# A gated delta rule layer with a mixture of experts on one core: gathers moved, GpSimd's first split behind the normalization, the last group's blocks sent earlier, new item orders in five iterations

## The reference

```python
St = St * jnp.exp(g_t)[..., None, None]
v_old = jnp.einsum('bhk,bhkv->bhv', k_t, St)
delta = (v_t - v_old) * b_t[..., None]
St = St + k_t[..., None] * delta[:, :, None, :]
o = jnp.einsum('bhk,bhkv->bhv', q_t, St)
```

## Time and profile before

| | |
|---|---|
| median of 3 runs | 1122.37 us (1120.64 to 1122.48) |
| the profiled execution | 1124.22 us |
| its span, first to last instruction | 1122.5 us |
| mean granted TensorE clock | 0.977 |
| PE busy | 1032.2 us (92%), 8190 matmuls |
| DVE busy | 809.2 us (72%) |
| ACT busy | 633.6 us (56%) |
| POOL busy | 524.9 us (47%) |
| the chain that ended last | PE 45%, DVE 10%, POOL 7%, ACT 5%, issue 5%, DMA 4% |

### The profile page before, as it was taken

The page is one execution under the profiler, slowest core; times in us unless marked ns, Lnnn a source line. Parts: engine busy times, 40 slices in busy tenths (PEclk is TensorE's granted clock), DMA queues, the critical chain, the costliest instruction groups (busy, mean ns, idle before and its releaser), DMA issues.

```text
span 1122.5 us, 22257 instructions
## 1 busy us (share of the span) xinstructions
PE 1032.2 (92%) x8190; PEld 791.8 (71%) x8190; DVE 809.2 (72%) x1469; ACT 633.6 (56%) x1176; POOL 524.9 (47%) x1140
## 2 busy tenths in 40 slices
PE   3999999987579999999999999999999999996987
PEld 3787666655367868677777878677777777684866
DVE  4632243429769898989888898989898888888444
ACT  2521222316537677676767676776767675674532
POOL 3331000006876465473837474563838383635620
PEclk9999999999869999999999999999999999998979
DMA  9941110014162423334152434234251524232121
GB/s 329 387 141 56 57 46 31 19 41 158 41 165 37 124 39 121 48 112 96 63 121 57 104 73 123 45 115 73 87 120 39 121 63 110 60 95 43 32 37 47
DMA packets 183513, 103.16 MB, mean 92 GB/s; under 512 B 155632, under 2 KB 169584, under 8 KB 180080
## 3 DMA queue, kind: packets, MB, share of 16 engines
q1 hardware_dynamic: 181872, 97.55, 31.7%
q0 software_dynamic: 1536, 4.20, 1.3%
HBM read 79.77 MB, written 21.95 MB: 91 GB/s over the span
## 4 chain that ended last, share of the span: by engine, by line
PE 45%; DVE 10%; POOL 7%; ACT 5%; issue 5%; DMA 4%; SPq 1%; DVEq 0%; ACTq 0%; POOLq 0%
PE rg L1512 7%; DVE nm L1276 5%; PE rg L1495 5%; PE rg L1479 4%; PE pj L1372 4%; PE pj L1373 4%; PE pj L1374 4%; POOL rows L1083 3%; POOL rows L1080 3%; PE rg L1487 2%; PE rg L1413 2%; PE rg L1496 2%; DVE shared_down_or_conv L1239 2%; ACT vn L1211 2%; ACT sqk L1165 2%
## 5 line engine op out<-in xcount | busy, mean ns | idle before, releaser
L1080 POOL TENSOR_TENSOR rows<-rows,shared_down_or_conv 128x126 f32<-128x126 f32 (+22 forms) x496 | 190.9, 385 | 240.5 <-DMA shared_down_or_conv<-n_scratch 202.8
L1239 DVE SCALAR_TENSOR_TENSOR shared_down_or_conv<-pj,taps,shared_down_or_conv 128x510 f32<-128x510 f32 x372 | 275.3, 744 | 26.4 <-ACT shared_down_or_conv L1128 17.5
L1083 POOL TENSOR_TENSOR rows<-rows 128x126 f32<-128x126 f32 (+22 forms) x496 | 197.0, 397 | 38.9
L1372 PE MATMUL pj<-xhi,whi 128*128 128x512 f32 x376 | 165.4, 440 | 7.6 <-DVE shared_down_or_conv L1239 3.9
L1276 DVE SCALAR_TENSOR_TENSOR nm<-rg,wneg,hidden_or_decays 128x512 f32<-128x512 f32 (+1 forms) x256 | 139.2, 608 | 16.4 <-PE rg L1415 16.2
L1373 PE MATMUL pj<-xlo,whi 128*128 128x512 f32 x376 | 150.7, 401 | 0.0
L1374 PE MATMUL pj<-xhi,wlo 128*128 128x512 f32 x376 | 150.5, 400 | 0.0
L1128 ACT ACTIVATE shared_down_or_conv<-pj,taps 128x512 f32<-128x512 f32 x124 | 85.3, 688 | 112.4 <-PE pj L1374 110.3
L1512 PE MATMUL rg<-wo,gated 128*128 128x256 f32 x512 | 132.2, 394 | 0.2 <-DVE nm L1276 0.2
L1512 PEld LDWEIGHTS rg<-wo,gated 128*128 128x128 f32 x512 | 95.4, 194 | 16.0 <-issue 2.2
L1372 PEld LDWEIGHTS pj<-xhi,whi 128*128 128x128 f32 x376 | 72.1, 192 | 46.5 <-issue 26.4
(11 more groups left out here) (216 smaller groups left out, 2033.8 us busy)
## 6 DMA issues: line engine op xcount, KB each, us to landing
hidden_or_decays<-eg_scratch SPq DMA_DIRECT2D x16, 1536.0 KB, 8.4
wraw<-w_heads SPq DMA_DIRECT2D x16, 776.0 KB, 4.4
w1a<-w_up SPq DMA_DIRECT2D x10, 1024.0 KB, 9.6
shared_down_or_conv<-n_scratch SPq DMA_DIRECT2D x32, 256.0 KB, 4.0
w2a<-w_down SPq DMA_DIRECT2D x8, 512.0 KB, 13.1
wo<-w_out SPq DMA_DIRECT2D x16, 256.0 KB, 2.7
n_scratch<-nm SPq DMA_DIRECT2D x64, 64.0 KB
rt_scratch<-shared_down_or_conv SPq DMA_DIRECT2D x32, 128.0 KB, 2.3
```

The costliest lines, as they stand in the source:

```text
L1080: gp.tensor_tensor(tmp, rb[:, 0:r, t:t + 1].to_broadcast([P, r, w]), nb[:, t:t + 1, t + 1:].to_broadcast([P, r, w]), ALU.mult).then_inc(el ...
L1083: gp.tensor_tensor(rb[:, 0:r, t + 1:], rb[:, 0:r, t + 1:], tmp, ALU.add).then_inc(elim, 1)
L1239: v.scalar_tensor_tensor(out=y, in0=it.pbank[item][:, :, 0:S - s], scalar=taps[par][:, piece(j)[0], KS - 1 - s:KS - s], in1=y, op0=ALU.mul ...
L1372: te.matmul(bank, whi[par][w], xhi[:, k, cols], start=(k == 0), stop=False)
```

## The change

1. POOL's first `split` waits for the end of DVE's normalization.
2. The 16 gathers go 5 ahead of `split_lo` of iteration -1, 3 behind it (ahead of elimination(0)), and 8 in iteration 0 behind `split_lo`, with the wait for all of them ahead of elimination(1).
3. SP's `blocks_out` is cut in two: the four writes (`blocks_out`) and the wait with the two fetches (`blocks_over`). In iteration NG - 2 the writes of group NG - 1 are issued inside `blocks_back(NG - 2)`, between `turned_back` and the wait ahead of `rows_back`. Elsewhere the order stays.
4. Iterations -1, 0, NG - 3, NG - 2 and NG - 1 get new lists of items for PE, ACT and DVE.

```diff
--- before.py
+++ after.py
@@ -303,6 +303,8 @@
                         gp.wait_ge(w_hi, s + 1)
                         if s:
                             gp.wait_ge(u_full, s * NS // ES)
+                        if s == 0:
+                            gp.wait_ge(dve, DVE_XN)
                         gp.tensor_tensor(w1lo[:], w1a[:, E - ES + s], w1hi[:].bitcast(F32), ALU.subtract).then_inc(w_lo, 1)
 
                     split(0)
@@ -852,37 +854,37 @@
             TAIL = {"SO", "OUT"}
             OWN = {
                 -1: (
-                    ("K0 K1 P4 K2 K3 P5 P6 P7 P0 P1 VT0 P2 VT1 VT2 P3 VT3").split(),
-                    ("P4 P5 W S4 P6 S5 SK P7 S6 P0 S7 P1 VT0 S0 P2 S1 P3 VT1 VT2 S2 S3 VT3").split(),
+                    ("K0 K1 K2 K3 P4 P5 P6 P7 P0 P1 VT0 VT1 VT2 P2 VT3 P3").split(),
+                    ("W P4 P5 S4 P6 S5 SK P7 S6 P0 S7 P1 S0 VT0 P2 VT1 S1 P3 VT2 VT3 S2 S3").split(),
                     ("K0 K1 K2 K3 P4 P5 P6 P7 P0 P1 P2 P3").split(),
                 ),
                 0: (
-                    ("P4 Z0 Z1 SQ P5 Z2 K0 Z3 P6 K1 P7 K2 K3 LA1 LA2 LB1 P0 LB2 P1 U1_0 U1_1 N21_0 N21_1 P2 U2_0 U2_1 "
-                     "VT0 P3 O0 O1 VT1 O2 O3 VT2 VT3").split(),
-                    ("E0 P4 Z0 SQ S4 P5 E1 Z1 P6 E2 E3 Z2 S5 SK W S6 LA1 P7 LA2 Z3 S7 LB1 LB2 P0 U1_0 U1_1 P1 U2_0 S0 "
-                     "U2_1 P2 S1 VT0 P3 O0 O1 VT1 O2 S2 S3 O3 VT2 VT3").split(),
-                    ("D0 D1 P4 D2 SQ P5 D3 K0 P6 K1 K2 K3 P7 MIX P0 N21_0 N21_1 P1 P2 P3 O0 O1 O2 O3").split(),
+                    ("Z0 Z1 P4 P5 SQ Z2 K0 P6 Z3 K1 K2 P7 P0 LA1 K3 LA2 LB1 P1 LB2 U1_0 U1_1 N21_0 N21_1 P2 U2_0 U2_1 "
+                     "VT0 P3 O0 VT1 O1 VT2 O2 O3 VT3").split(),
+                    ("E0 Z0 P4 SQ Z1 S4 P5 S5 E1 P6 E2 W Z2 E3 SK S6 Z3 P7 LA1 LA2 S7 LB1 LB2 U1_0 U1_1 P0 P1 S0 U2_0 P2 "
+                     "U2_1 VT0 S1 O0 P3 O1 VT1 O2 S2 O3 VT2 S3 VT3").split(),
+                    ("D0 P4 D1 D2 P5 SQ D3 K0 P6 K1 K2 P7 K3 MIX N21_0 N21_1 P0 P1 P2 O0 P3 O1 O2 O3").split(),
                 ),
                 NG - 3: (
-                    ("SO P4 Z0 SQ K0 K1 OUT0 Z1 Z2 Z3 OUT1 P5 OUT2 OUT3 LA1 P6 P7 K2 K3 LA2 OUT4 P0 LB1 OUT5 P1 LB2 P2 "
-                     "U1_0 OUT6 U1_1 N21_0 N21_1 U2_0 U2_1 OUT7 VT0 P3 O0 O1 VT1 O2 VT2 O3 VT3").split(),
-                    ("SQ P4 Z0 SO E0 E1 Z1 Z2 S4 W P5 Z3 S5 E2 P6 LA1 P7 E3 LA2 SK LB1 S6 P0 LB2 U1_0 S7 P1 U1_1 U2_0 S0 "
-                     "P2 S1 U2_1 VT0 O0 P3 S2 VT1 O1 O2 VT2 O3 VT3 S3").split(),
-                    ("SO D0 D1 SQ P4 K0 K1 D2 OUT0 P5 OUT1 OUT2 OUT3 D3 K2 K3 P6 P7 OUT4 OUT5 P0 OUT6 N21_0 N21_1 P1 P2 "
-                     "OUT7 O0 P3 O1 O2 O3").split(),
+                    ("SO Z0 P4 Z1 SQ Z2 K0 OUT0 K1 OUT1 Z3 OUT2 P5 P6 P7 LA1 K2 OUT3 LA2 K3 LB1 OUT4 OUT5 LB2 P0 OUT6 "
+                     "U1_0 U1_1 N21_0 P1 N21_1 U2_0 P2 U2_1 P3 VT0 OUT7 VT1 O0 O1 O2 O3 VT2 VT3").split(),
+                    ("SQ Z0 E0 Z1 P4 Z2 E1 SO Z3 P5 W E2 LA1 S4 E3 LA2 P6 LB1 S5 LB2 P7 S6 U1_0 P0 U1_1 SK S7 P1 U2_0 S0 "
+                     "P2 S1 U2_1 P3 VT0 VT1 S2 O0 O1 O2 O3 VT2 S3 VT3").split(),
+                    ("D0 SO D1 SQ P4 K0 OUT0 OUT1 D2 K1 D3 OUT2 P5 K2 OUT3 K3 P6 OUT4 OUT5 P7 OUT6 N21_0 P0 N21_1 P1 P2 "
+                     "OUT7 P3 O0 O1 O2 O3").split(),
                 ),
                 NG - 2: (
-                    ("P4 Z0 SO SQ K0 K1 Z1 K2 OUT0 K3 P5 LA1 P6 OUT1 LA2 OUT2 OUT3 OUT4 LB1 OUT5 OUT6 LB2 P7 Z2 Z3 U1_0 "
-                     "OUT7 U1_1 N21_0 N21_1 U2_0 U2_1 VT0 VT1 VT2 O0 O1 O2 O3 VT3").split(),
-                    ("P4 E0 SQ SO E1 E2 S4 E3 P5 Z0 Z1 LA1 P6 S5 LA2 LB1 S6 LB2 P7 U1_0 S7 SK U1_1 U2_0 U2_1 Z2 O0 VT0 "
-                     "VT1 O1 VT2 Z3 O2 O3 VT3").split(),
-                    ("D0 P4 SO D1 SQ D2 K0 K1 D3 K2 K3 OUT0 P5 OUT1 OUT2 P6 OUT3 OUT4 P7 OUT5 OUT6 OUT7 N21_0 N21_1 O0 "
+                    ("P4 Z0 SO SQ Z1 P5 K0 K1 K2 K3 LA1 Z2 OUT0 P6 OUT1 OUT2 Z3 OUT3 OUT4 LA2 P7 LB1 OUT5 OUT6 LB2 U1_0 "
+                     "U1_1 N21_0 N21_1 OUT7 U2_0 U2_1 VT0 VT1 O0 O1 O2 VT2 VT3 O3").split(),
+                    ("P4 SQ SO E0 Z0 E1 S4 Z1 P5 E2 E3 LA1 S5 P6 Z2 Z3 LA2 SK LB1 LB2 U1_0 U1_1 U2_0 P7 S6 U2_1 S7 VT0 "
+                     "O0 O1 VT1 O2 VT2 VT3 O3").split(),
+                    ("D0 D1 SO P4 SQ D2 D3 K0 K1 K2 K3 P5 OUT0 P6 OUT1 OUT2 OUT3 OUT4 OUT5 OUT6 N21_0 N21_1 P7 OUT7 O0 "
                      "O1 O2 O3").split(),
                 ),
                 NG - 1: (
-                    ("Z0 Z1 Z2 SO OUT0 OUT1 OUT2 OUT3 LA1 OUT4 LA2 OUT5 LB1 OUT6 OUT7 LB2 Z3 U1_0 U1_1 N21_0 N21_1 U2_0 "
+                    ("Z0 SO Z1 Z2 OUT0 OUT1 OUT2 OUT3 LA1 OUT4 LA2 OUT5 OUT6 LB1 OUT7 LB2 Z3 U1_0 U1_1 N21_0 N21_1 U2_0 "
                      "U2_1 O0 O1 O2 O3").split(),
-                    ("Z0 SO Z1 LA1 LA2 LB1 Z2 LB2 U1_0 U1_1 U2_0 U2_1 O0 Z3 O1 O2 O3").split(),
+                    ("SO Z0 Z1 LA1 LA2 LB1 LB2 U1_0 U1_1 U2_0 U2_1 Z2 O0 O1 Z3 O2 O3").split(),
                     ("SO OUT0 OUT1 OUT2 OUT3 OUT4 OUT5 OUT6 OUT7 N21_0 N21_1 O0 O1 O2 O3").split(),
                 ),
                 NG: (
@@ -985,6 +987,8 @@
                         rows_of = nm[par][C32 * q:C32 * (q + 1)].rearrange("p b e -> p (b e)").rearrange("p (m s) -> p m s", s=EC)
                         sp.dma_start(n_dram[:, q].rearrange("m i x -> i m x"), rows_of[:, :, first:first + C32]
                                      ).then_inc(blocks_out_sem, 16)
+
+                def blocks_over(n):
                     at_least(sp, blocks_out_sem, 64, n, 64)
                     at_least(sp, rt_out, 32, n, 0)
                     for h in range(2):
@@ -1014,6 +1018,8 @@
 
                     turned_back(0, t64[0:C32, :, :, 0:HR], turned_in)
                     turned_back(2, tc2, turned_in)
+                    if n == NG - 2:
+                        blocks_out(n + 1, 1 - it.odd)
                     sp.wait_ge(r_out, 32 * n + 32)
                     rows_back(1, back_odd)
                     rows_back(3, back_odd)
@@ -1030,7 +1036,9 @@
                     if "LA1" in it.items_a:
                         blocks_back(b, it)
                     if "K3" in it.items_v:
-                        blocks_out(b + 1, 1 - it.odd)
+                        if b != NG - 2:
+                            blocks_out(b + 1, 1 - it.odd)
+                        blocks_over(b + 1)
                         if "W" in it.items_a:
                             load_decays(b + 2)
                     if "OUT7" in it.vpos and "O3" in it.vpos:
@@ -1098,15 +1106,17 @@
                                               in_offset=bass.IndirectOffsetOnAxis(ap=posi[:, i:i + 1], axis=0)).then_inc(gathered, 16)
 
                 def run(it):
+                    if it.b == -1:
+                        gather(range(0, 5))
                     if "W" in it.items_a:
                         split_lo(it.b + 2, it.odd, it)
                     if it.b == -1:
-                        gather(range(0, 4))
+                        gather(range(5, 8))
+                    elif it.b == 0:
+                        gather(range(8, 2 * NT))
+                        gp.wait_ge(gathered, 2 * NT * 16)
                     if "K3" in it.items_v:
                         eliminate(it.b + 1, it)
-                    if it.b == -1:
-                        gather(range(4, 2 * NT))
-                        gp.wait_ge(gathered, 2 * NT * 16)
 
                 for it in ITERATIONS:
                     run(it)
```

## The result

The changed kernel takes **1110.96 us** (median of 9 runs, 1103.69 to 1117.22); the kernel before, beside it, 1121.16 us (9 runs, 1117.74 to 1123.74). The ratio is 0.990, 95% interval 0.9875 to 0.9924: 10.2 us or 1.0% faster. The profiled execution took 1110.96 us too, with a span of 1109.1 against 1122.5.

A forecast was written before the change was run, and what follows sets the result against it. Elimination, its transfers and PE hold each other with under 1 us of slack, PE having real holes only at both ends. Terms 4.2 + 1.7 + 0.2 + 5.4 = 11.5 us off 1122.37 give 1110.9 us, range 1104 to 1117.

The forecast's parts named there:

- setup: Start of the kernel, up to PE's first transpose: the wait for the normalization gains 4.2 us.
- front: Gathers and group 0, up to LA1(1): new gather places and item orders gain 1.7 us.
- tail: Groups 13 to 15: new orders and early blocks gain 0.2 us at LA1(15) and 5.4 us behind it.
- Part 1: Setup: GpSimd's wait removes the eighth normalization's stall, PE starts at 13.4 instead of 17.54; 4.2 us, bounds 0 and 4.4.
- Part 2: Gathers around elimination(0): LA1(0) 6.8 us behind SyncE's issue, last gather at 317.7 instead of 319.1, mixing ends 325, not 329.1.
- Part 3: Group 0's order: elimination(1) 1 us later, LA1(1) at 362.2 if PE is there; 1.7 us gained, bounds -1 and +3.5.
- Part 4: Group 13: P6 and P7 fill the 2.49 us hole ahead of LA1; blocks go out 3.1 us earlier, LA1(14) at 1031.8.
- Part 5: Group 14: early blocks bring elimination(15) 3.8 us earlier, PE stalls 3.45 us before VT0; LA1(15) gains 0.2 us.
- Part 6: From LA1(15) to LB2: upper instead of lower clock if no hole stands directly ahead; 5.4 us, bounds 0 and 6.
- (a): Rival, tail keeps its hole: clock stays low through LA1(15), or P7's stall feeds it; 1114 to 1117 us, chance 0.20.
- (b): Rival, tail: P7's stall smaller, LA1(15) at 1076 to 1077, upper clock, front gives 3; 1104 to 1107 us, chance 0.20.
- (c): Rival, setup: the wait changes nothing because the long eighth instruction has another cause; 1115 us, chance 0.05.

The follow-up runs named there:

- front only: Kernel before with only the gathers' new places and the new item orders of iterations -1 and 0, without GpSimd's wait; ratio 0.9991 to the kernel before.
- wait only: Kernel before with only GpSimd's wait for the normalization ahead of its first split; 1134.56 us against 1136.28, ratio 0.9975.
- P7's tap early: Changed kernel with P7's tap on ScalarE between LB1 and LB2 in group 14, P7 on VectorE ahead of N21_0; 1104.73 and 1108.22 us (0.9863, 0.9871 of before).
- the changed kernel's second trace: Profiled execution of the unaltered changed kernel, run again beside other experiments; that run took 1107.68 us, ratio 0.9879 to the kernel before.
- K ahead in 13: P7's tap early plus, in group 13, K2 and K3 ahead of LA1 and P6 and P7 behind it; 1123.18 us, ratio 0.9893 to the kernel before.

## Why the prediction was right

The forecast named the three places that pay, setup, front and tail, and the traces bear out what happens at each, the clock behind LA1(15) above all. That 1110.96 lies on 1110.9 is in part luck. In the pair of traces the forecast's own terms give 4.23 + 0.56 - 1.21 + 5.31 = 8.9 us of its 11.5, and the other 4.5 us of the 13.4 lie in stretches where it put nothing. The medians show 10.2 us, and the parts one by one 7.5.

- **Part 1, the wait, 4.2 us:** 4.23, and 4.3 with the wait alone. What I missed is that the same code wins the race by itself at times, as front only did; in the times the wait is worth 2.8 (interval 0.3 to 5.3).
- **Part 2, the gathers:** LA1(0) 6.70 us behind the issue (6.8); the last gather in time with 310.2, which is 316.3 on the scale of before (317.7).
- **Part 3, group 0, 1.7 us:** 0.56 in the pair, 2.0 to 2.7 over all traces. The size was right, the mechanism not: *"elimination(1) is 1 us later ... LA1(1) at 362.2, if PE is there"*. Elimination(1) came 1.4 us earlier and its end 2.3, and PE was not there: it was 4.3 us late, at the lower clock for up to 22.5 us behind LA1(0). Over all traces the gain is made ahead of LA1(0), by the gathers, 3.6 to 4.4 us (1.6 to 2.8 beside 1136), and behind it some is given back.
- **Part 4, group 13, 3.1 us:** 2.89; blocks 8.43 us behind LA1(13) (8.2).
- **Part 5, group 14:** the stall of 3.45 us is there with 3.38 and is P7's tap, as its removal shows. *"3.8 us earlier"* for elimination(15) is 2.45, since the fetch keeps waiting behind the rows. It did no harm, because PE sets LA1(15), as forecast. The clock's fall behind the stall, put at 1 us, cost 1.5 to 2.9 where it came (17.74, 19.13 and 18.93 us from VT0 to LA1(15) against 16.25; in the first VT took 1.97 for 1.09 and O 4.74 for 4.09) and nothing where it didn't.
- **Part 6, behind LA1(15), 5.4 us:** 5.31 in the pair and 4.4 to 5.0 in the other four traces of the changed tail, at clock 1.00 in every trace without a hole ahead of LA1(15), 0.85 with one of 1.24 us (wait only), and 0.50 in the five with one of 3.5 us or more.
- **The rivals:** (a) in its first form didn't come, for no trace of the changed tail has a hole ahead of LA1(15), though P7's stall did feed the lower clock in three of five. (b) needed a smaller stall, and it was 3.38 us in all five. The runs of the changed kernel reach from 1103.7 to 1117.2, the ends of both; what made single ones fast or slow is not shown. (c) fell with the wait alone.

The 2.30 us of the router and the 2.44 us of the loop in the profiled pair are chance: the loop takes 609.3 to 617.1 us in the fourteen traces, and the two groups don't part (old and new fronts alike). A single group shows how, group 8 in P7's tap early and in the changed kernel's second trace (length; busy time of PE, PEld, DVE, ACT, POOL; clock; DMA share; GB/s):

```profile
712.14:765.73 53.59, 51.15 (x456) 39.77 (x457) 45.19 (x81) 35.95 (x68) 29.72 (x68) 0.97 0.33 83
```

```profile
710.59:761.03 50.44, 49.53 (x456) 39.05 (x457) 44.24 (x79) 35.93 (x68) 29.72 (x67) 1.00 0.34 88
```

## What to carry to other kernels

Read every wait at the place that you speed up against the engine that comes next: at LA1(15) the early blocks made elimination earlier for nothing, since PE set it, and what was left to gain lay in PE's own stall. A hole costs its length and the work at the lower clock behind it: the 3.5 us ahead of LA1(15) cost 5.3 us more behind it, and the 7.9 us opened there by K ahead in 13 took back more, in its trace, than the 6 us that closing the hole of group 14 had given. A VectorE instruction that lies beside a long GpSimd subtraction deserves a look wherever one is found: the change removed one such stall of 4.2 us, and another of the same size stands in half of the traces. And one pair of traces carries chance of several us: cut it into stretches and look which of them repeat before a term is believed.

## What was unexpected of the hardware

- A VectorE instruction beside a GpSimd subtraction can come out either way with the same code: 4590 ns in one trace, 416 ns at most in another, and the subtraction 4.72 and 5.01 us. In both, the subtraction's recorded start lies 0.2 to 0.3 us ahead of the eighth normalization's, so the order of the records doesn't tell who wins. With the recorded start behind it, by GpSimd's wait, no stall came in ten traces.
- The router's 32 matmuls, 0.8 us behind the transposes, took 7.02 us in six traces of fourteen, and 4.19 to 5.15 us in the other eight. In the six, the row of the granted clock reads 1.00 over these matmuls, and over the 128x512 ones behind them, which take 0.63 us and not the 0.40 of the upper level; so at the start of a program durations tell the level, and the row doesn't.
- The clock fell behind a stall of the same 3.38 us, amid the same order of work, in three traces of five. What decides it is open.
